# A perceiver layer on one core: two units' probabilities moved in halves of the keys, and a second group in another order

## The reference

```python
q = (layernorm(x) @ Wq)            # 16 heads of 128
k, v = ctx @ Wk, ctx @ Wv          # 2048 context rows, 8 key/value heads, each shared by 2 query heads
scores = q @ k.T / sqrt(128); scores = where(mask, scores, -inf)
x = x + softmax(scores) @ v @ Wo                       # cross attention
x = x + causal_attention(layernorm(x))                 # 16 heads, 4 key/value groups, 128 keys
x = x + moe(layernorm(x))                              # one shared expert, 16 experts of which 2 count
```

## Time and profile before

| | us |
|---|---|
| median of 3 runs | 346.92 (346.61 to 347.24) |
| the profiled execution's own time | 347.99 |
| its span, first to last instruction | 346.2 |
| PE busy in it | 332.2 (96%) |
| DVE, ACT, POOL busy | 271.6, 231.3, 231.7 |

### The profile page before, as it was taken

How to read it: one execution, slowest core, us unless ns; L and a number is a source line. 1 busy time by engine, 2 the same in 40 slices (tenths; PEclk the granted TensorE clock), 3 DMA queues, 4 the chain that set the end, 5 groups by cost and what they waited for, 6 DMA issues and landing times.

```text
span 346.2 us, 6876 instructions
## 1 busy us (share of the span) xinstructions
PE 332.2 (96%) x2251; PEld 301.1 (87%) x2251; DVE 271.6 (78%) x466; ACT 231.3 (67%) x414; POOL 231.7 (67%) x142
## 2 busy tenths in 40 slices
PE   7999988999999999999999998999999999899995
PEld 5887867999999999999999987999898897699995
DVE  2776888898988988989889889576458845579996
ACT  2799449586597687777767777794246676266761
POOL 3666709799499599599598596748425778417550
PEclk9999999999999999999999999999999999999999
DMA  6711558866886885895795886992141040504530
GB/s 191 259 32 38 115 132 197 220 152 153 221 188 152 205 202 130 207 209 122 176 209 116 197 182 177 206 323 79 48 139 45 2 151 1 153 1 135 171 105 31
DMA packets 32565, 49.98 MB, mean 144 GB/s; under 512 B 5536, under 2 KB 23072, under 8 KB 32544
## 3 DMA queue, kind: packets, MB, share of 16 engines
q1 hardware_dynamic: 32544, 49.72, 57.2%
HBM read 20.08 MB, written 0.26 MB: 59 GB/s over the span
## 4 chain that ended last, share of the span: by engine, by line
PE 81%; DVE 6%; ACT 4%; SPq 3%; issue 2%; POOL 1%; DMA 1%; DVEq 0%; POOLq 0%; ACTq 0%
PE bank L584 12%; PE bank L585 11%; PE bank L586 11%; PE pair L584 11%; PE pair L585 11%; PE pair L586 11%; SPq L279 3%; PE bank L788 2%; PE bank L965 1%; ACT probs L1210 1%; PE pair L958 1%; PE pair L950 1%; ACT first_pT L1282 1%; DVE resid L1934 1%; PE bank L958 1%
## 5 line engine op out<-in xcount | busy, mean ns | idle before, releaser
L444 POOL TENSOR_TENSOR pT<-pT,pT_hi 128x1024 fp32r<-128x1024 f32 x54 | 129.5, 2423 | 36.0 <-ACT pT_hi L1220 35.9
L1210 ACT ACTIVATE probs<-probs,lowest 128x2048 f32<-128x2048 f32 x32 | 64.3, 2010 | 23.3 <-DVE lowest L1588 23.3
L1220 ACT ACTIVATE pT_hi<-pT 128x1024 fp32r<-128x1024 f32 x56 | 57.6, 1055 | 12.8 <-DMA pT<-ctx_raw 8.7
L584 PE MATMUL bank<-pT_hi,ctx_lo 128*128 128x256 f32 x224 | 63.9, 285 | 1.7 <-POOL pT L444 1.6
L585 PE MATMUL bank<-pT,ctx_hi 128*128 128x256 f32 x224 | 64.2, 287 | 0.0
L586 PE MATMUL bank<-pT_hi,ctx_hi 128*128 128x256 f32 x224 | 63.6, 284 | 0.0
L584 PE MATMUL pair<-ctxT_hi,qk_lo 128*128 128x512 f32 x128 | 52.2, 408 | 0.0
L586 PE MATMUL pair<-ctxT_hi,qk_hi 128*128 128x512 f32 x128 | 50.1, 391 | 0.0
L1588 DVE CUSTOM_DVE_ANT_0 probs<-pair,mask_bias,lowest 128x1024 f32<-128x1024 f32 x32 | 40.9, 1279 | 11.6 <-PE pair L586 10.9
L585 PE MATMUL pair<-ctxT_lo,qk_hi 128*128 128x512 f32 x128 | 50.0, 390 | 0.0
L444 POOL TENSOR_TENSOR ctx_lo<-ctx_raw,ctx_hi 128x512 fp32r<-128x512 f32 (+1 forms) x19 | 31.5, 1671 | 24.0 <-DVE route L1927 9.3
(11 more groups left out here) (266 smaller groups left out, 835.8 us busy)
## 6 DMA issues: line engine op xcount, KB each, us to landing
pT<-blocks SPq DMA_DIRECT2D x112, 128.0 KB, 2.3
pT<-ctx_raw SPq DMA_DIRECT2D x112, 128.0 KB, 2.3
ctx_raw<-ffn_experts_gate_up_dram SPq DMA_DIRECT2D x16, 256.0 KB, 2.9
wq<-in_L_xattn_Wq_dram SPq DMA_DIRECT2D x8, 256.0 KB, 2.8
ctx_raw<-in_ctx_dram SPq DMA_DIRECT2D x8, 256.0 KB, 6.2
wo<-in_L_xattn_Wo_dram SPq DMA_DIRECT2D x8, 256.0 KB, 3.1
blocks<-in_L_attn_w_dense_dram SPq DMA_DIRECT2D x4, 512.0 KB, 4.4
ctx_raw<-_L_ffn_experts_down_dram SPq DMA_DIRECT2D x16, 128.0 KB, 2.4
```

Source lines behind the costliest of these rows:

```text
L444: pool.tensor_tensor(dst, src, hi.bitcast(F32), ALU.subtract).then_inc(ready, 1)
L584: pe.matmul(dst, w[1], x[0], start=start, stop=False)
L1210: act.activation(probs[:, j], probs[:, j], ACT.Exp, bias=lowest[:, p, j, 1:2], scale=-1.0, accum_out=den[:, p, j:j + 1]).then_inc(exps, 1)
L1220: act.activation(hi_slot(c), chunk(p, c).bitcast(F32), ACT.Copy).then_inc(pT_hi_ready, 1)
```

## The change

Three things change.

1. For the units (0, 1) and (6, 1), SP moves the probabilities in two halves of the keys: 16 DMAs of 64 KB for keys 0 to 1023, which count on a new semaphore `half_landed`, and then 16 for keys 1024 to 2047, which count on `landed[1]`. ACT's rounds of chunks 0 and 1 wait for the first half, those of chunks 2 and 3 for the second. All other units are moved as before. The first pass of SP's loop is written out for that.
2. In the last group, ACT rounds chunks 0 and 1 of unit (6, 1) ahead of `oT_unit(12)`, as the other groups do.
3. In group 1 (and at one place of group 0) the order written by hand is another one, on PE, ACT, DVE and POOL.

The diff, cut:

```diff
+        def move_half(eng, a, q, half, done):
+            keys = slice(half * NBLK // 2, (half + 1) * NBLK // 2)
+            eng.dma_start(pT[1][LN * q:LN * (q + 1), a, :, keys].bitcast(F32),
+                          blocks[1][LN * a:LN * (a + 1), q, :, keys]).then_inc(done, 16)
...
+            def move_halves(g):
+                after(sp, av, 8 * g)
+                sp.wait_ge(turned, 2 * (2 * g + 1) + 2)
+                for half, done in ((0, half_landed), (1, landed[1])):
+                    for r in range(QD):
+                        for q in range(QD):
+                            move_half(sp, q, (q + r) % QD, half, done)
...
-            with sp.Fori(1, G - 3) as g:
+            move_halves(0)
+            load_wk(3)
+            move_blocks(1, 0)
+            load_wq(4)
+            load_o(1)
+            with sp.Fori(2, G - 3) as g:
...
-                move_blocks(g - 1, 1)
+                if g == G - 1:
+                    move_halves(g - 1)
+                else:
+                    move_blocks(g - 1, 1)
...                                                        # POOL
-            rest_wq(3)
             for c in range(4):
                 rest_p(1, 1, c)
+            rest_wq(3)
...                                                        # PE, group 1
             score(1, 4)
-            y_project(0, 0)
-            score(1, 5)
             q_project(2, 0)
             q_project(2, 1)
             wk_transpose(2)
+            y_project(0, 0)
+            score(1, 5)
+            pe.wait_ge(ctx_lo_ready, B)
+            attend(1, 1, 0)
             score(1, 6)
-            out_project(0, 0)
             q_fold(2)
             score(1, 7)
-            pe.wait_ge(ctx_lo_ready, B)
-            attend(1, 1, 0)
             attend(1, 1, 1)
+            out_project(0, 0)
...                                                        # ACT, p_round
-                if c == 0:
+                if isinstance(g, int) and p == 1 and g in (0, G - 2):
+                    if c == 0:
+                        act.wait_ge(half_landed, 256 if g == 0 else 512)
+                    if c == 2:
+                        act.wait_ge(landed[p], 256 * (g + p))
+                elif c == 0:
...                                                        # ACT, group 0
+            q_copy(1)
+            wkT_copy(1)
             copy_first(6)
             copy_first(7)
-            q_copy(1)
-            wkT_copy(1)
...                                                        # DVE, group 1
-            yT_rest(0)
+            q_rest(2)
+            wkT_rest(2)
             denominators(1, 1)
             mask_pair(1, 5)
-            q_rest(2)
-            wkT_rest(2)
+            yT_rest(0)
```

More of the change, by code:

```diff
@@ L238, in perceiver_layer @@
         landed = [sem(f"landed{b}") for b in range(B)]
+        half_landed = sem("half_landed")
         pT_hi_ready, pT_lo_ready = sem("pT_hi_ready"), sem("pT_lo_ready")
@@ L1254, in group @@
                 o_round(g - 1)
-                if last:
-                    oT_unit(2 * (g - 1), 0)
                 p_round(g - 1, 1, 0)
                 p_round(g - 1, 1, 1)
-                if not last:
-                    oT_unit(2 * (g - 1), 0)
+                oT_unit(2 * (g - 1), 0)
                 p_round(g - 1, 1, 2)
@@ L1340, in _ @@
             oT_unit(0, 0)
-            wq_round(3)
-            yT_copy(0)
             p_round(0, 1, 0)
@@ L1345, in _ @@
             wkT_copy(2)
+            yT_copy(0)
             p_round(0, 1, 1)
+            wq_round(3)
+            p_round(0, 1, 2)
             exp_row(1, 2)
             fold_copy(2, 0)
-            p_round(0, 1, 2)
             p_round(0, 1, 3)
```

## The result

The changed kernel takes 364.8 us (median of four runs, 364.2 to 366.15) against 346.76 of the kernel before on the same chip: a ratio of 1.0523, 95% interval 1.049 to 1.0556, 18.0 us slower. The profiled execution took 365.2 us, its span 363.4, 17.2 more than before. The prediction had the sign and 11.85 of these us; the time is above its range.

The account below looks back on a forecast made before the run. The prediction took PE to bound the kernel, busy 332.2 us, 96% of the span. Delays of 5.15 and 6.7 us, together 11.85, added to the median of 346.92 gave 358.8 us, range 346.0 to 362.0.

Parts of the forecast that it names:

- The price of an issue: On SP's queue: a half-size move costs 0.634 us to issue, as a whole one, so 32 take twice as long; chance 0.56.
- the catch-up: On the DMA engines: four moves landed in 2.04 us, 0.51 each, so 0.634 is not the transfer's floor.
- cheap issues: Rival on SP's queue: issues cost 0.47 to 0.51 us, like loads back to back; 349 to 352 us, chance 0.19.
- bytes: Rival: bytes set the issue period, 0.32 us for a half; both places win, 342.0 us, chance 0.19.
- 31 x period - 12.2: Approximate formula for the delay at the last group as a function of the issue period.
- the turning point: Issue period of 0.43 to 0.44 us at which both places change sign together.
- Place one: Groups 1 and 2: unit (1, 0)'s moves start 6.65 us late behind the halves; less 1.50 slack, PE is 5.15 late.
- Place two: Last group: the second half delays ACT's third round and the exponential behind it, so PE's turning transposes start 6.7 us late.
- which covers it: Last set of pT[0] on SP: starts 3.4 us later than PE's delay, covered by 3.3 us of slack before its first reader.
- the sum: Both places' delays of PE added: 5.15 + 6.7 = 11.85 us.
- PE's work, which the change leaves as it is, plus PE's waits: Premise on the whole time: PE is busy 332.2 us, 96% of the span, unchanged, so only its waits can move.
- the time would stay at 346.9: Case in which the first half is not earlier and no longer queue stands behind it: no change from the kernel before.

Follow-up runs that it names:

- third_round_late: The changed kernel with ACT's third rounding of units (0, 1) and (6, 1) put behind the exponentials of row 2: 365.6 us, ratio 1.0499 to the kernel before.
- halves_old_order: The kernel before with the halves alone at both places and no line of the order moved: 365.2 us, ratio 1.0528.
- gap_worked: Whole moves, new order with two scores, a fold and three copies put back, plus q_project(2,1) and wk_transpose(2) behind score(1,5): 348.5 us, ratio 1.0027 to the kernel before.

## Why the prediction was too low

**The price of an issue: right.** 0.634 was taken; the 32 take 21.49 us, 0.67 each with the slow ones, and two experiments confirm that neither bytes nor rows set it. Nor was the period the transfer's, as the prediction took from the catch-up: while the halves go out, the DMA engines are 0.44 to 0.46 busy at the same period. No rival came about: not cheap issues, not bytes. (One side sum of the rivals is off: "31 x period - 12.2" gives 7.5 at 0.634, where the text works out 6.7; only the turning point hangs on it.)

**Place one, 5.15 us forecast, 8.5 measured.** The chain of steps is the one that the prediction gave. Its first `attend` of unit (1, 0) came 7.4 us late and not 5.15. Of the 2.2 more, 0.9 is the later start of the set (59.10 for 58.20) and 1.0 its slower end: ACT's round followed the start by 12.9 us, and by 11.9 in the earlier trace rows. Most of both are slow issues, below. PE's wait itself, 2.37 us, stands one step ahead of the one forecast, at `y_project`, whose `oT_hi` ACT copies behind the first two rounds; it ends at 75.01, sooner than POOL's first chunk at 75.48, and 0.3 more is that `y_project`, at half clock. Behind it the rest of that half clock, up to 78.4, cost another 1.1 us.

**Place two, 6.7 us forecast, 6.4 measured ahead of the transposes, and 2.3 behind them.** The wait was right. SP's stall came again 8.75 us into the set (8.83 before), but as 1.31 us and not 2.39; that smaller delays made up for most of the rest, so that the 32 take 21.73 us for the 22.0 reckoned, is luck. The step "which covers it" on the last set's slack of 3.3 us (its own numbers leave it 0.1 short) holds only while the transposes are late, as `third_round_late` shows.

**The step that failed is the sum,** and under it the premise that the time is "PE's work, which the change leaves as it is, plus PE's waits". 5.15 + 6.7 counts PE's waits and takes every matmul behind them at the price of the kernel before. PE's idle time grew by 11.3 us, close to the 11.85; PE's busy time grew by 5.9, at half clock behind the waits, and no term held that. That the 11.3 comes so close is partly luck: SP was 1.9 us later than forecast, and slower matmuls filled some 2.2 us that would have been waiting. Of the 5.9, about 3.7 lay on the path, 1.4 at place one and 2.3 at place two; the rest was waited for anyway. With these 3.7 and the 1.9 by which SP was later than forecast, less 0.3 at place two, the sum is 17.2; without the 3.7 it is 13.45, which gives 360.4 us, inside the range. The rest of the 18.0 lies between profiled executions and medians.

**A second step was wrong, but cost nothing here:** that a moved line of the order could cost no more than its own duration, under 2.38 us, and with it that without the longer queue "the time would stay at 346.9". The moved lines were priced one by one; the new wait ahead of `attend(1, 1, 0)` was seen, but taken as time won before and lost again, without the half clock behind it. With whole moves the order costs 3.9, of which 1.6 to 2.0 is the clock behind a wait that it made out of three. The rest fits the waits of the two profiles (4.65 us for 3.31 at place one, 1.93 for 1.63 in the last group), but no run tells these apart; some 0.7 may be the last group's. With the halves it cost nothing: `halves_old_order` takes as long as the changed kernel.

## What to carry to other kernels

Before a transfer is split, price the issue on the queue and not the bytes: here twice the issues were twice the time, and all that stands behind them in the queue was late. On TensorE a wait can have a second price, the matmuls behind it at half clock: here three waits of 3.3 us in all went without it, and one of 4.65 did not. When a forecast adds up waits of the bounding engine, look at what the profile's clock row does behind the longest wait it already has.

## What was not expected of the hardware

An issue on SP's queue at times takes 1.3 to 2.4 us and not 0.6. In the changed kernel two issues from 38.30 on take 2.17 us together, 0.64 being the usual one; SP's timeline, and the DMA view of 38.9 to 40.4 us:

```profile
38.30 2.17 SPq L286 DMA_DIRECT2D pT<-blocks  x2
```

```profile
q8 instruction: 1, 0.02, 4.7%
...
pT<-blocks SPq DMA_DIRECT2D x1, 64.0 KB, 2.9
```

One packet of the instruction queue lies in that stretch, and one in 68.0 to 69.9, where the last issue of unit (1, 0)'s set is slow. In the kernel before, one lies in 207.7 to 210.1, where an issue takes 2.39 us. That they delay the issue is inferred from their coincidence.

The length of a wait alone did not tell whether the clock fell: behind 2.15 us in `third_round_late` the next stretch is at 1.00, behind 1.85 in `gap_worked` at 0.61. Before, the longest wait of the cross attention, 1.67, left it alone; no length below which a wait is safe can be read from these rows.
